# GNN message passing with a residual layer norm: GpSimd takes the norm of every third node chunk in place of its pauses

## What is computed

```
m   = relu(concat(x[src], x[dst], edge_attr) @ W1 + b1) @ W2 + b2          # per edge, 128 wide
m   = m * sigmoid(concat(m, edge_weight) @ Wa + ba)
out = layernorm(x + segment_sum(m, dst, 100000))                            # per node, no scale or shift
```

## Time and profile before

| | |
|---|---|
| time, three runs | median 699.24 us (695.41 to 699.42) |
| the profiled execution | 698.01 us, of which the span from first to last instruction is 696.3 us |
| busy | PE 400.3 us, PE weight load 286.0, DVE 460.3, ACT 426.6, POOL 460.0 |
| granted TensorE clock, mean | 0.801 |
| DMA | 159.3 MB, mean 229 GB/s; software queue (POOL's) 14.7% of 16 engines, hardware queue (SP's) 54.9% |
| issue to landing, median | nodes<-x 6.8 us, out<-nodes 4.3, rows_src<-x,src_list 4.3, out<-stash 3.5 |
| DVE work from SBUF to SBUF (busy us) | nodes norm rows 68.5, acc 43.7, stash<-acc,rows_dst 20.3, pick 21, place 23, near norm rows 12.8, head 7 |

### The profile page before, as it was taken

The page is one execution under the profiler, slowest core; times in us unless marked ns, Lnnn a source line. Parts: engine busy times, 40 slices in busy tenths (PEclk is TensorE's granted clock), DMA queues, the critical chain, the costliest instruction groups (busy, mean ns, idle before and its releaser), DMA issues. The chain is left out here.

```text
span 696.3 us, 7976 instructions
## 1 busy us (share of the span) xinstructions
PE 400.3 (57%) x1902; PEld 286.0 (41%) x1902; DVE 460.3 (66%) x1555; ACT 426.6 (61%) x1089; POOL 460.0 (66%) x473
## 2 busy tenths in 40 slices
PE   1776884656738547384472967194744647498200
PEld 0454653434526336263351645062523535376100
DVE  4877886996694848678386779668575764555300
ACT  0354997699667937495373968586773769455200
POOL 7666665665667666675664766666756777677772
PEclk9998997787787959697696889697885977789555
DMA  6979788999885957768677679878485755731310
GB/s 159 366 225 330 250 308 286 331 297 334 291 288 153 316 181 264 261 193 289 192 243 261 217 251 302 284 251 297 154 304 179 243 179 166 200 94 47 102 48 18
DMA packets 79874, 159.30 MB, mean 229 GB/s; under 512 B 13970, under 2 KB 48086, under 8 KB 79826
## 3 DMA queue, kind: packets, MB, share of 16 engines
q1 hardware_dynamic: 65106, 129.47, 54.9%
q0 software_dynamic: 14720, 29.32, 14.7%
HBM read 99.75 MB, written 59.95 MB: 229 GB/s over the span
## 5 line engine op out<-in xcount | busy, mean ns | idle before, releaser
L777 ACT ACTIVATE nodes<-nodes,sc 128x128 f32<-128x128 f32 (+1 forms) x462 | 184.0, 485 | 0.0
L758 ACT ACTIVATE turned<-turn_ps 128x512 f32<-128x512 f32 x147 | 81.1, 591 | 167.8 <-PE turn_ps L878 92.9
L669 POOL DMA_INDIRECT rows_dst<-x,dst_list x132 | 129.5, 981 | 74.1 <-DMA rows_src<-x,src_list 35.7
L679 POOL DMA_INDIRECT out<-stash,row_idx x132 | 136.1, 1031 | 63.6 <-issue 35.6
L658 POOL DMA_INDIRECT rows_src<-x,src_list x132 | 129.1, 978 | 64.3 <-issue 36.4
L904 PE MATMUL hid_ps<-turned,w 128*128 128x512 f32 x294 | 158.5, 681 | 2.7 <-ACT turned L758 2.6
L1187 DVE BATCH_NORM_STATS2 stats<-nodes 128x6 f32<-128x256 f32 (+1 forms) x358 | 133.5, 418 | 17.0 <-DMA nodes<-x 17.0
L878 PE MATMUL turn_ps<-ident,rows_src 128*128 128x128 f32 x196 | 36.5, 317 | 109.3 <-DMA rows_src<-x,src_list 102.6
L914 PE MATMUL msg_ps<-w2x,hid 128*128 128x129 f32 x392 | 71.5, 341 | 36.6 <-ACT hid L763 36.6
L904 PEld LDWEIGHTS hid_ps<-turned,w 128*128 128x128 f32 x294 | 62.2, 228 | 65.0 <-issue 59.2
L914 PEld LDWEIGHTS msg_ps<-w2x,hid 128*128 128x128 f32 x392 | 65.0, 250 | 40.3 <-ACT hid L763 40.3
(11 more groups left out here) (139 smaller groups left out, 477.2 us busy)
## 6 DMA issues: line engine op xcount, KB each, us to landing
nodes<-x SPq DMA_DIRECT2D x62, 704.0 KB, 6.8
out<-nodes SPq DMA_DIRECT2D x62, 704.0 KB, 4.3
attr_in<-edge_attr SPq DMA_DIRECT2D x49, 256.0 KB, 5.4
near_dst<-line SPq DMA_DIRECT2D x16, 256.0 KB, 6.3
near_x<-x SPq DMA_DIRECT2D x20, 192.0 KB, 4.4
near_x<-x SPq DMA_DIRECT2D x24, 128.0 KB, 4.5
out<-near SPq DMA_DIRECT2D x4, 704.0 KB, 6.6
rows_src<-x,src_list POOLq DMA_INDIRECT x132, 4.3
```

Source lines behind the costliest of these rows:

```text
L669: pool.indirect_dma_start(out=rows_dst[:, i % RING, j, :], out_offset=None, in_=x[:, :], in_offset=bass.IndirectOffsetOnAxis(ap=column(dst ...
L679: pool.indirect_dma_start(out=out[:, :], out_offset=bass.IndirectOffsetOnAxis(ap=column(row_idx, i, j), axis=0), in_=stash[:, list_slot(i) ...
L758: act.activation(turned[:, k % 2, c], turn_ps[:, c], ACT.Copy).then_inc(turned_ready, 1)
L777: return act.activation(row, row, ACT.Identity, scale=sc[0:parts, b % 2, 0, col:col + 1], bias=sc[0:parts, b % 2, 1, col:col + 1])
```

## The change

`group_steps` lists the step k of each of the 115 groups, and `third_rows_places` picks for each of the 21 batches the even-numbered groups that belong to steps 2b + 3 and 2b + 4. Behind each of them POOL now normalizes a part of the third chunk's 11 rows (5 and 6 where there are two such groups, 3, 4 and 4 where there are three). There are 47 such places, from group 6 to group 98. The pause in the second group after such a place is left out; the pauses in groups 2, 4 and 6 and from 102 on stay. ACT and DVE no longer touch the third chunks, and DVE's `batch_scales(b)` also waits for normed of the third chunk of batch b - 2, whose scales lie in the half of `sc` that it writes.

```diff
-ACT_ROWS = (7, 7, 8)
+ACT_ROWS = (7, 7)
...
+def group_steps():
+    at = [0, 1, 0, 1]
+    for k in range(2, K):
+        at += [k] * (1 + is_list(k) + len(SCATTERS.get(k, ())))
+    return at
+
+def third_rows_places():
+    at, places = group_steps(), {}
+    for b in range(21):
+        behind = [n + 1 for n, k in enumerate(at) if n % 2 and k in (2 * b + 3, 2 * b + 4)]
+        for q, n in enumerate(behind):
+            places[n] = (b, ROWS * q // len(behind), ROWS * (q + 1) // len(behind))
+    return places
...
+THIRD_ROWS = third_rows_places()
...
             def pause(j):
                 landed, value, behind = latest
-                if j == behind and groups[0] % PAUSE == PAUSE - 1:
+                if j == behind and groups[0] % PAUSE == PAUSE - 1 and groups[0] - 1 not in THIRD_ROWS:
                     pool.wait_ge(landed, value)
 
             def group_begun(landed, value, behind):
                 groups[0] += 1
                 latest[:] = landed, value, behind
+                if groups[0] in THIRD_ROWS:
+                    third_rows(*THIRD_ROWS[groups[0]])
+
+            def third_rows(b, low, high):
+                c = chunk_of_batch(b, 2)
+                u, n = c % SLOTS, chunk_parts(c)
+                pool.wait_ge(scale_ready, 2 * (b + 1))
+                for r in range(low, high):
+                    col = node_column(b, 2, r)
+                    last = pool.tensor_scalar(nodes[0:n, u, r, :], nodes[0:n, u, r, :], sc[0:n, b % 2, 0, col:col + 1],
+                                              sc[0:n, b % 2, 1, col:col + 1], ALU.mult, ALU.add)
+                if high == ROWS:
+                    last.then_inc(normed[u], 2)
...
                 if k % 2:
                     norm_chunk(b, 0)
-                elif k:
-                    norm_chunk(b, 2)
...
                 wait(dve, scale_free, b - 1)
+                if b > 1 and chunk_of_batch(b - 2, 2) is not None:
+                    c = chunk_of_batch(b - 2, 2)
+                    dve.wait_ge(normed[c % SLOTS], 2 * (c // SLOTS + 1))
...
-                under = norm_rows(b - 1, (2,)) + near_norm_rows(b - 1) if k % 2 == 0 else []
+                under = near_norm_rows(b - 1) if k % 2 == 0 else []
```

## The result

The changed kernel takes 730.91 us in the median of four runs (729.81 to 733.62), against 698.12 us for the kernel before in the same session: 1.048 times as long, with a 95% interval of 1.044 to 1.053. It is slower. The profiled execution took 730.99 us, 33.0 more than the profiled one before. The forecast was 717 us in a range of 686 to 745.

What follows compares the result with a forecast made beforehand. The prediction took POOL's own queue of indirect DMAs, issue times and landing waits to bound the kernel. From 698.0 us, less 77.5 for pauses, plus 88.9 for rows and 8 for DVE's interference, it forecast 717 us, range 686 to 745.

Steps and rivals of the forecast that it cites:

- Sign: Whole kernel: slower by over 1%, chance 0.58; within 1% had 0.20, a gain of over 1% had 0.22.
- likeliest case: POOL's rows with collisions cost 0.365 to 0.50 us each, giving 705 to 736 us around 717; chance 0.42.
- What bounds the kernel: POOL's own queue of 460 indirect DMAs, issue times and landing waits is the span; no other engine paces POOL.
- Term 1, the pauses: In POOL's queue, 47 pauses for landings of its own transfers go, saving 77.5 us.
- Term 2, the rows: 231 norm rows come onto POOL at 0.385 us each, adding 88.9 us (ends 56.6 and 115.5).
- Term 3, DVE in the way: DVE's SBUF to SBUF instructions hold up POOL's instructions, adding 8 us (4 to 13).
- What costs nothing: POOL's wait for scales, third chunks' later stores and reloads (some 12 us to spare), and ACT's and DVE's lost rows.
- faster: Rival: POOL's rows run near the affine_select's 0.245 us, giving 680 us, up to 690; chance 0.22.
- No change: Rival: POOL's rows and collisions come to about 0.335 us each, equal to the pauses removed, 692 to 705 us; chance 0.20.
- Landings as the limit: Rival: POOL's transfers can't be queued ahead, so pause time returns as longer DMAs or waits, 741 us; chance 0.12.
- The loop: Rival: third chunk's store, reload, statistics and scale come later than POOL asks for the scale, 752 us; chance 0.04.

## Why the prediction was right, and where it missed

Sign and mechanism were right, and the time lies in the range: POOL's queue is the sum, and the removed pauses were worth less than the rows. The time came out 14 us above the forecast, a loss of 33 us where 19 was forecast, near the upper end of the likeliest case (705 to 736). Term by term:

- **What bounds the kernel:** right. POOL's waits for PE stay under 1 us in the changed kernel, and each run that kept rows on POOL moved the time by what it did to POOL's queue. Without the pauses the queue is no longer quite alone: 9 to 15 us of waiting for DVE's stash appear.
- **Term 1, the pauses:** 77.5 us forecast, 77.1 in the profile. The term holds in full only with the rows beside it: without any rows in their place the 47 gave 67 us.
- **Term 2, the rows:** this is the step that failed in size. "I take 0.385 us, ACT's pace for the same operation" gave 88.9 us; undisturbed rows took 0.434, 100.3 us in all. The nearest row in content was on another engine, while the price of a constant on POOL was what mattered. The select's 0.245 plus two constants, the 0.415 that the prediction worked out with the price that the Trainium skill gives for a small read (GPSIMD Engine Reference, section 7), was nearer, and its 724 us nearer to the result.
- **Term 3, DVE in the way:** 8 us taken, 13.7 measured, just above the bound of 13 us. That the bound came so near is partly luck: it counted the chunks' norm rows among the holders, and taking them off DVE changed nothing.
- **Not forecast:** the DMA behind rows starts 0.14 us sooner, 6.6 us less in all, which hid a part of the misses above. With 11.4 for the rows, 5.7 for the delays, 1.8 of idle time, 0.7 for DMAs and 0.4 for the pauses that makes 13.4 of the 13.6 us between 717.4 and 731.0.
- **What costs nothing:** right. POOL never waited for a scale, though DVE's wait for reloaded chunks rose by 44 us.
- **The rivals:** "faster" falls, since a row that reads its two constants is far from the select's pace; with none the kernel would have been faster (683.9). "No change" falls too: it needed 0.335 us for a row and its collisions, and they took 0.494. Landings as the limit falls with the runs without pauses. The loop did not decide.
- **Two slips in the sums:** 0.50 us rows with 13 us of collisions give 698.0 - 77.5 + 115.5 + 13 = 749, and not the 745 that the range is said to take in. And landings of 10 us each lengthen the loop by 8.9 us, which is less than the 12 it had to spare. Neither bears on the result.

What the prediction did not do was to price the two halves of the change apart. Its own first term said that leaving out the 47 pauses alone would give some 77 us. They gave 67, and the best kernel of this study is the one without any pauses.

## What to carry to other kernels

When one queue is the span, a pause in it that orders no data is worth trying without, before anything is put in its place: work moved onto the bounding queue is added to the span, and relief on the other engines is worth nothing as long as that queue waits for none of them. A change with two halves of opposite sign should be priced, and run, as two. Price an instruction from its parts on its own engine (here a bare operation and each constant it reads) before taking the same operation's pace from another engine.

## What the runs showed of the hardware that was not expected

- Each per-partition constant read from SBUF costs a GpSimd tensor_scalar of 128 x 128 f32 about 0.083 us: 0.268, 0.350 and 0.434 us with none, one and two.
- The pauses for landings bought no time: without any of them the four groups of DMA_INDIRECT instructions are as long as with them (979 to 1028 ns against 978 to 1031), and POOL's instructions take 0.95 us each in a stretch with the DMA engines 97% busy.
- An indirect DMA that follows a compute instruction on POOL starts 0.16 us after it, behind another indirect DMA 0.30 us.
- A run of back-to-back norm rows on POOL is not delayed by DVE's norm rows of the same kind (114.0 us with them and without) and delays them instead (0.52 us on average and up to 0.93 for one of 0.34).
- DVE's `place` (TENSOR_SCALAR, one input tile) and stash addition (two input tiles) stand beside the stretches of POOL's rows that are too long: 12.4 us of the delays lie in the 21 of 47 stretches that overlap one of the two. This is read from overlaps alone.
